# Eight layers on one core: the schedule of a mixture-of-experts refinement is rearranged

## The reference, cut to what matters

```python
logits = gelu(xf @ w_r1 + b_r1) @ w_r2 + b_r2          # 8 experts
top_p, top_i = top_k(softmax(logits), 2); top_p /= sum(top_p)
v = 0; integrated = xf                                 # xf: layer-normed x
for _ in range(2):
    ctx = concat([integrated, v])                      # 256 wide
    shared = inl(gelu(ctx @ w_s1 + b_s1) @ w_s2 + b_s2, integrated, v)
    routed = [inl(gelu(ctx @ w1[e] + b1[e]) @ w2[e] + b2[e], integrated, v) for e in top_i]
    x_next = sw * shared.x + (1 - sw) * sum(top_p * routed.x)
    v_next = sw * shared.v + (1 - sw) * sum(top_p * routed.v)
    halt = sigmoid(gelu(x_next @ w_h1) @ w_h2)
    refined = gelu(x_next @ w_f1) @ w_f2
    integrated += halt * refined * integration_weight
    v = v_next
# inl(ctrl, x, v): alpha, beta, gate = sigmoid, softplus, sigmoid of three thirds of ctrl
#   v' = alpha*v - beta*(x - mu);  x' = x + 0.1*gate*v'
```

## Time and profile before

| what | value |
|---|---|
| runs, us | 1178.99, 1173.0, 1180.49 (median 1178.99) |
| the profiled execution's own time | 1176.08 us |
| its span in the profile | 1174.0 us |
| mean granted TensorE clock | 0.899 of full |
| PE busy over the span | 953.2 us (81%) |
| DVE / ACT / POOL busy | 735.9 / 583.3 / 413.9 us |
| the layer that changes | about 128.7 to 445 us of the span |

### The profile page before, as it was taken

How to read it: one execution, slowest core, us unless ns; L and a number is a source line. 1 busy time by engine, 2 the same in 40 slices (tenths; PEclk the granted TensorE clock), 3 DMA queues, 4 the chain that set the end, 5 groups by cost and what they waited for, 6 DMA issues and landing times. The chain is left out here.

```text
span 1174.0 us, 26596 instructions
## 1 busy us (share of the span) xinstructions
PE 953.2 (81%) x10777; PEld 622.7 (53%) x10777; DVE 735.9 (63%) x2026; ACT 583.3 (50%) x956; POOL 413.9 (35%) x426
## 2 busy tenths in 40 slices
PE   4999798998999986998897791887566676579997
PEld 2677433443333433777676390555355565456776
DVE  3587757547455564654475133368899999636764
ACT  3365475535555344554563550477545655325442
POOL 4320300000000011677101656246678878623341
PEclk9799799999999998999897796889778887699998
DMA  6000000000000008000000132100000000000001
GB/s 270 1 3 3 19 1 0 1 1 0 1 1 1 0 1 297 3 3 3 2 3 2 55 92 56 72 2 1 1 2 3 2 3 2 2 2 2 2 2 37
DMA packets 15431, 27.92 MB, mean 24 GB/s; under 512 B 1104, under 2 KB 13264, under 8 KB 14544
## 3 DMA queue, kind: packets, MB, share of 16 engines
q1 hardware_dynamic: 14288, 24.14, 5.7%
q0 software_dynamic: 1024, 2.10, 0.6%
HBM read 20.33 MB, written 5.90 MB: 22 GB/s over the span
## 5 line engine op out<-in xcount | busy, mean ns | idle before, releaser
L1332 PE MATMUL l0f_ctl<-l1f_in,l0f_in 128*128 128x512 f32 x320 | 145.5, 598 | 0.0
L133 POOL TENSOR_SCALAR row_var_eps<-row_mean_var 128x12 f32<-128x12 f32 (+2 forms) x16 | 3.8, 236 | 355.9 <-DVE row_mean_var L128 355.1
L556 DVE TENSOR_REDUCE l_neg_max<-l_ring 128x4 f32<-128x512 f32 x128 | 82.1, 683 | 63.5 <-PE l_ring L418 62.9
L515 ACT ACTIVATE l_probs<-l_scores 128x1024 f32<-128x1024 f32 x64 | 65.5, 1024 | 82.2 <-PE l_scores L426 82.2
L2672 ACT COPY l2f_blocks_sb<-l2f_right_t_sb 32x1024 f32<-32x1024 f32 x64 | 66.8, 1044 | 66.2 <-PE l2f_given_ps L2602 33.1
L1332 PEld LDWEIGHTS l0f_ctl<-l1f_in,l0f_in 128*128 128x128 f32 x320 | 61.4, 192 | 71.1 <-issue 69.8
L2602 PE MATMUL l2f_given_ps<-l2f_blocks_sb,l2f_left_t_sb 128*32 128x128 f32 x1024 | 47.1, 360 | 31.3 <-ACT l1f_in L2678 21.8
L706 POOL TENSOR_TENSOR l_squares<-l_exps 128x1024 f32<-128x1024 f32 x32 | 60.6, 1893 | 27.9 <-ACT l_exps L961 27.9
L1053 DVE TENSOR_REDUCE l_neg_max<-l_scores 128x8 f32<-128x1024 f32 x32 | 39.2, 1225 | 44.3 <-PE l_scores L758 44.3
L2602 PEld LDWEIGHTS l2f_given_ps<-l2f_blocks_sb,l2f_left_t_sb 128*32 128x32 f32 x1024 | 41.2, 146 | 45.9 <-issue 45.4
L376 POOL TENSOR_SCALAR_AFFINE_SELECT l_probs<-l_probs 128x1024 f32<-128x1024 f32 x32 | 34.9, 1092 | 62.5 <-ACT l_probs L515 62.5
(11 more groups left out here) (458 smaller groups left out, 2625.7 us busy)
## 6 DMA issues: line engine op xcount, KB each, us to landing
l1f_in<-in_l1f SPq DMA_DIRECT2D x1, 4580.0 KB, 13.6
l0f_in<-in_l0f SPq DMA_DIRECT2D x1, 2302.5 KB, 8.6
l0f_in<-in_l2f SPq DMA_DIRECT2D x1, 2080.5 KB, 19.3
l1f_in<-in_l2u SPq DMA_DIRECT2D x1, 2048.0 KB, 7.8
sorted_rows<-first_in SPq DMA_DIRECT2D x1, 1856.0 KB, 11.5
l1f_sorted<-sorted_rows SPq DMA_DIRECT2D x7, 256.0 KB, 4.8
expert_rows<-l1f_sorted SPq DMA_DIRECT2D x7, 256.0 KB, 2.2
x_in<-in_x SPq DMA_DIRECT2D x1, 1024.0 KB, 4.7
```

What stands on the lines that cost most here:

```text
L515: nc.scalar.activation(probs[c % 2][:, 2 * pair:2 * pair + 2], scores2[:, :, :, :, :], ACT.Exp, scale=SCORE_SCALE).then_inc(exp_done, 1)
L556: ring.free(V.tensor_reduce(out, score_bank(b, half, g), AX.X, ALU.max, negate=True), ("score", b, half, g))
L1332: return nc.tensor.matmul(out, lhs, rhs, start=start, stop=stop)
```

## The change

It does the following, in the second layer alone:

1. POOL waits until all rows are normalised before it clears `choice`.
2. `split_bias` takes one branch at a time (128 x 384): branch 0 before the ranking, branch 1 after the first `order`. TensorE waits for each branch's own half.
3. The stage "spread" is cut in two: "spread" keeps the index rows and `expand`, a new stage "share" has the weight rows.
4. The table moves: in phase 0 only group 0 is hidden and chosen at step 0; its spread comes at step 1; choosing group 1, the shares of group 0, hiding and spreading group 1 come at step 2; the shares of group 1 at step 3. In phase 3 group 2 is spread at step 7 alone; its shares, the hiding of group 3 and the turn back of (1,0) come at step 8. In phase 4 the shares of group 3 come at step 3, ahead of the ask.
5. The two sums into v leave `fresh` and come after x_next, as `add_to_v`, which also counts `beta_used[0]` after the first sum and `beta_used[1]` after the second.

```diff
     BESIDE = {
-        (0, 0): (("route", 0, 0), ("rank", 0, 0), ("hide", 0, 0), ("hide", 0, 1), ("choose", 0, 0), ("choose", 0, 1),
-                 ("spread", 0, 0)),
-        (0, 2): (("spread", 0, 1),),
+        (0, 0): (("route", 0, 0), ("rank", 0, 0), ("hide", 0, 0), ("choose", 0, 0)),
+        (0, 1): (("spread", 0, 0),),
+        (0, 2): (("choose", 0, 1), ("share", 0, 0), ("hide", 0, 1), ("spread", 0, 1)), (0, 3): (("share", 0, 1),),
...
-        (3, 7): (("finish", 1, 0), ("spread", 0, 2)), (3, 8): (("hide", 0, 3),),
-        (4, 2): (("spread", 0, 3),), (4, 3): (("ask", 1, 1),), (4, 4): (("answer", 1, 1),), (4, 5): (("finish", 1, 1),),
+        (3, 7): (("spread", 0, 2),), (3, 8): (("share", 0, 2), ("hide", 0, 3), ("finish", 1, 0)),
+        (4, 2): (("spread", 0, 3),), (4, 3): (("share", 0, 3), ("ask", 1, 1)), (4, 4): (("answer", 1, 1),), (4, 5): (("finish", 1, 1),),
...
-        "choose": ("choice",), "spread": ("index0", "index1", "weight0", "weight1"),
+        "choose": ("choice",), "spread": ("index0", "index1"), "share": ("weight0", "weight1"),
...
             norm.pool(pool)
+            norm.wait_rows(pool, B)
             nc.gpsimd.memset(choice[:, :, :, :], 0.0).then_inc(ready, 1)
...
-                if n == 0 and r == 0 and part == BETA:
-                    pe.wait_ge(b2_split, 1)
+                if n == 0 and r < 2 and part == BETA:
+                    pe.wait_ge(b2_split, r + 1)
...
-            def split_bias():
-                b2, b2_left = w["b2"][:, :, :], chosen[0][:, 0, 0:2, 0:384]
...
+            def split_bias(r):
+                b2, b2_left, part, split = w["b2"][:, r, :], chosen[0][:, 0, r, 0:384], b2_part[:, r, :], b2_bf[:, r, :]
...
                         if c == 0:
-                            split_bias()
+                            split_bias(0)
                             rank(it, 0)
                             rank(it, 2)
                         order(it, c)
+                        if c == 0:
+                            split_bias(1)
...
-                    ins = TT(vs, vs, beta[r], ALU.add)
-                    if r == 0:
-                        own(ins)
-                ins.then_inc(v_made, 1)
+
+            def add_to_v(n, c):
+                vs = v[c % 2][:, :]
+                TT(vs, vs, gated[BETA][0][:, :], ALU.add).then_inc(beta_used[0], 1)
+                dve.wait_ge(beta_used[0], n + 1)
+                TT(vs, vs, gated[BETA][1][:, :], ALU.add).then_inc(v_made, 1)
+                dve.wait_ge(v_made, c + 1)
+                dve.sem_inc(beta_used[1], 1)
...
-                source, used = (gated[ALPHA][r], alpha_used[r]) if it else (gated[BETA][r], beta_used[r])
                 ctl.wait_freed(dve, (n, r, GATE), 0)
-                STT(gate[r], gate[r], 1.0, source[:, :], ALU.add, ALU.mult).then_inc(used, 1)
-                dve.wait_ge(used, seen(it, c) + 1 if it else n + 1)
+                if it:
+                    STT(gate[r], gate[r], 1.0, gated[ALPHA][r][:, :], ALU.add, ALU.mult).then_inc(alpha_used[r], 1)
+                    dve.wait_ge(alpha_used[r], seen(it, c) + 1)
+                else:
+                    own(STT(gate[r], gate[r], 1.0, gated[BETA][r][:, :], ALU.add, ALU.mult))
...
                     dve.wait_ge(next_made, n + 1)
+                    if not it:
+                        add_to_v(n, c)
```

More of the change, by code:

```diff
@@ L1365, in spread, with share_out, spread_rows @@
             def spread(it, c):
+                spread_rows("spread", it, c)
+            def share_out(it, c):
+                spread_rows("share", it, c)
+            def spread_rows(stage, it, c):
                 work.wait_freed(pe, f"choice_{it}{c}", 0)
-                for k, name in enumerate(WORK_OF["spread"]):
+                for k, name in enumerate(WORK_OF[stage], 2 * (stage == "share")):
                     name = f"{name}_{it}{c}"
@@ L1415, in stages @@
                     if stage != "rank":
-                        {"route": route_all, "hide": hide, "choose": choose, "spread": spread,
+                        {"route": route_all, "hide": hide, "choose": choose, "spread": spread, "share": share_out,
                          "ask": ask, "answer": answer, "again": again, "finish": finish}[stage](it, c)
@@ L1499, in stages @@
                     if stage not in ("rank", "finish"):
-                        {"route": route_all, "hide": hide, "choose": choose, "spread": spread, "ask": ask,
-                         "answer": answer, "again": hide}[stage](it, c)
+                        {"route": route_all, "hide": hide, "choose": choose, "spread": spread, "share": share_out,
+                         "ask": ask, "answer": answer, "again": hide}[stage](it, c)
             A(sw_tanh[:, :], w["shared_weight"][:, :], ACT.Tanh, scale=0.5).then_inc(sw_made, 1)
@@ L1545, in _ @@
             pre(TS(half_b[:, :], w["b_h2"][:, :], 0.5, None, ALU.mult))
-            def split_bias():
-                b2, b2_left = w["b2"][:, :, :], chosen[0][:, 0, 0:2, 0:384]
-                own(V.tensor_copy(b2_part[:, :, :], b2))
-                own(TS(b2_bf[:, :, :], b2_part[:, :, :], w["split_rows"][:, 0:1], None, ALU.mult))
+            def split_bias(r):
+                b2, b2_left, part, split = w["b2"][:, r, :], chosen[0][:, 0, r, 0:384], b2_part[:, r, :], b2_bf[:, r, :]
+                own(V.tensor_copy(part, b2))
+                own(TS(split, part, w["split_rows"][:, 0:1], None, ALU.mult))
                 for s in (1, 2):
[L1552 to L1555, removed]
+                    own(TT(b2_left, b2 if s == 1 else b2_left, part, ALU.subtract))
+                    own(V.tensor_copy(part, b2_left))
+                    own(STT(split, part, w["split_rows"][:, s:s + 1], split, ALU.mult, ALU.add))
                 dve.sem_inc(b2_split, 1)
```

## The result

Eight runs of each kernel: 1166.51 us in the median (1163.28 to 1170.82) against 1177.94 (1173.0 to 1180.49). The ratio is 0.9909 with a 95% interval of 0.9889 to 0.9929, so the change saves 8.4 to 13.1 us. The forecast was 8.9 us.

A forecast was written before the change was run, and what follows sets the result against it. TensorE was taken as the bound, busy 287.6 of the layer's 310 us. Savings of 1.6 + 0.6 + 1.6 + 5.1 = 8.9 us from the 1178.99 median gave 1170.1, say 1170 us, range 1162 to 1177.

The forecast's parts named there:

- Part 1: Opening: clearing `choice` behind the normalised rows brings the routing and logits forward by 1.62 us, bounds 0 and 1.8.
- Part 2: Opening: bias split in halves on DVE costs 0, with 0.4 us or more of slack; bounds 0 to 1 us late.
- more than 0.3 a sign of error: Opening: the forecast is wrong if DVE reads the logits more than 0.3 us after they are made.
- Part 3: Opening's new order: first hide to first chosen control takes 18.1 us instead of 19.1; net 0.6, bounds -1.0 and 2.6.
- Part 4: Sums into v behind x_next, phases 0 and 4: 0.55 and 0.65 us gained, perhaps another 0.4; bounds 0.5 and 3.5.
- Part 5: Phases 3 and 4, new order: 7.6 us removed, new waits added; net 5.1 gained, bounds 3 and 6.6.
- The two new waits: TensorE waits for weight copies: 1.0 us before the hide at step 8, 1.5 before the ask at (4,3).
- The slower rival: Opening: idle before the hide of group 1 lowers the clock between 148 and 165; -6.9 us, 1186 us, chance 0.04.

The follow-up runs named there:

- ask-first trace: The changed kernel with the shares of group 3 behind the ask at (4,3) instead of ahead of it: layer 309.37 us, ratio 0.9922 to the kernel before.
- the turn back alone: The changed kernel with only the turn back of (1,0) ahead of the spread at (3,7) again: ratio 0.9994 to the kernel before, layer 311.02 us.

## Why the prediction was right

The measured 1166.51 lies in the range and 3.5 us below the forecast; the saving of 8.9 us stands beside 8.77 in the layer. But the sum came out better than its terms, and part of that is luck: a gain and a loss by the clock that were in no term, 2.5 us and 1.7, partly cancel. Point by point:

- *Part 1, 1.62 us:* L185 gave back 1.66 us, and at equal clock (the ask-first trace) the first hide starts 10.21 us into the layer instead of 11.90, 1.69 sooner. Undone, 1.4 at the first chosen control. Right. The price named behind it, a stalled cast, is there: 1.42 against 0.36.
- *Part 2, cost 0 with 0.4 us of slack:* right in effect, though DVE reads the logits 0.9 us after they are made (138.09, against 137.15). I had called more than 0.3 a sign of error. It came from logits that were 1.2 us quicker at the higher clock; what counts is the choice at 143.16, before 143.46. (The prediction's 143.9 for the choice is a slip: 139.1 and 5.1 make 144.2, still ahead of 145.6.) That part 1 needs the halving in the new order is shown: undone, 1.5 us are lost.
- *Part 3, 0.6 us net:* 0.85 by undoing it.
- Parts 1 to 3 together: forecast 2.2. At equal clock it is 28.71 against 31.04, less 0.44: 1.9. The clock wasn't wholly equal: it rose 15.6 us into the layer in the kernel before and 15.2 in the ask-first one, so of the earlier work more ran low, and the hide of group 0 took 7.28 us against 6.59. With these 0.7 us it would be 2.6. In the profiled execution it was 4.35, and **2.46 of them are the clock**: the routing and logits ran at 0.93 where before they ran at 0.50. Windows of both, 134 to 138 us, the changed kernel and then the ask-first one, with the same code there (the kernel before has 0.50 in that window too):

```profile
134.00:138.00 4.00, 3.22 (x42) 1.64 (x34) 3.70 (x8) 1.46 (x2) 1.17 (x3) 0.93 0.00 0
```

```profile
134.00:138.00 4.00, 3.20 (x36) 2.04 (x28) 3.65 (x8) 1.12 (x2) 1.02 (x3) 0.50 0.00 0
```

- *Part 4, 0.55 and 0.65 with perhaps 0.4:* 0.5 (4.99 us ahead at the control after the ask, against 4.51 before it) and 0.97. Right, and so was the reason, Abs waiting for the first sum: doubling the tile took that wait away. Undone, phase 5 shows 0.4 by the waits; the rest of its 0.97 is the ask that no longer ran at the lower clock. The wait for the Gelu was to be over 2 us and is 1.97.
- *Part 5, 5.1 us:* 4.67 (7.95 us ahead after the ask of phase 4, against 3.28 before the spread of phase 3). The two new waits were put at 1.0 and 1.5. Counted as there, from start to start, they are 1.0 (280.95 less 279.52, less two rows) and 1.9; the profile's own 0.83 and 1.73 leave out the modelled ends. So the wait ahead of the ask was put 0.4 too low, and the ask itself, 0.3 us quicker (2.78 against 3.09), was put at 0.5. The clock's share is as forecast (1.69), the rest 3.0 instead of 3.4, and of that the turn back alone gives 3.1 (its own experiment, above): the shares' step brings nothing.
- *The slower rival:* **its mechanism struck, at another place.** Nothing fell between 148 and 165, where I put it (clock 1.00). But after the ask of phase 1 eight passes took 5.29 us instead of 3.60, 1.7 us lost. I had argued that the like couldn't happen, because idles of 2.40 and 1.05 had kept the clock at 1.00; here 1.02 and 1.97 let it fall. The step that failed is this use of one row as a rule, and the earlier trace rows already spoke against it: the idle of 2.55 in phase 4's x_next was followed by an ask at the lower clock, 4.84 us against 3.25.
- The ledger of the profiled pair: 4.35 + 0.48 - 1.70 + 4.67 + 0.97 = 8.77. Without the two clock items it is 8.0, or 8.7 with the 0.7 above, against 8.9 forecast. What the ledger can't tell is how much the kernel before varies, since it was traced once; other kernels varied by 2.5 us in the opening alone.

## What to carry to other kernels

In a layer held by TensorE, look for the bank that a slow reader holds: one group's turn back placed ahead of a spread cost 4.3 to 4.7 us, 1.3 to 1.7 of them by the clock that fell behind the wait, more than all reordering at the start. When work is moved behind a result, list who waits for its buffer too: with the two sums out of the way the wait for x_next fell by 1.4 us in phase 1, and the wait for the Gelu behind it grew by 0.9, because ACT waited for their tile. And compare a stretch at equal clock, by a second trace of the same code, before a gain is credited to an edit.

## What was not expected of the hardware

- The granted clock of the same stretch of code, with the same waits before it, differs between kernels. In this layer it repeated for one kernel: three traces of the changed one had it at 307.96, 307.98 and 307.93 us, low in the same places; in the stretch behind it it did not (188.5, 185.1, 185.0). Kernels with the same opening had the first hide of group 1 start 20.3 to 20.6 us into the layer or 22.8 to 23.0. The waits at the first ask, 1.02 and 1.97, were followed by a low stretch in the changed kernel (the eight passes took 5.29 us) and by eight passes in 3.60 us in the ask-first one.
- Clearing 128 x 2048 on POOL held up DVE steps on SBUF operands in both places: two of the 13 normalising steps then, one cast now. The Trainium skill, "SBUF — State Buffer", section "Who interferes with whom", says that of GpSimd and a DVE instruction in a two-port mode the one that issues second is blocked for the whole of the other's instruction. The cast, which began 0.6 us into the clearing and ended 0.21 us after it, agrees in the main, though alone it takes 0.36; which mode it ran in no trace here shows.
